# Routing by 16-bit comparisons with the row innermost, on running numbers that GpSimd writes first

## The reference

```
def _L0_ffn_ref(x, Wr, br, W1, b1, W2, b2):
    logits = jnp.einsum('bsd,de->bse', x, Wr) + br
    _, top_idx = jax.lax.top_k(logits, 2)
    mask = jnp.any(top_idx[..., None] == jnp.arange(num_experts), axis=-2)
    weights = jax.nn.softmax(jnp.where(mask, logits, NEG_INF), axis=-1)
    for e in range(num_experts):
        h = jax.nn.relu(jnp.einsum('bsd,dh->bsh', x, W1[e]) + b1[e])
        y = jnp.einsum('bsh,hd->bsd', h, W2[e]) + b2[e]
        out = out + y * (weights[:, :, e] * mask[:, :, e])[:, :, None]

def _L1_ffn_ref(x, router_W, router_b, W1, b1, W2, b2):
    probs = jax.nn.softmax(x @ router_W + router_b, axis=-1)
    gates = jax.nn.one_hot(jnp.argmax(probs, axis=-1), N_EXPERTS) * probs
    h = jax.nn.relu(jnp.einsum('bsd,edf->besf', x, W1) + b1[:, None, :])
    y = jnp.einsum('besf,efd->besd', h, W2) + b2[:, None, :]
    out = jnp.einsum('bse,besd->bsd', gates, y)
```

## Time and profile before

| | us |
|---|---|
| median of 3 runs | 1454.43 |
| lowest and highest of them | 1447.27, 1460.71 |
| the profiled execution's own time | 1442.47 |
| its span in the trace, first to last instruction | 1440.8 |
| routing of layer 0, from its first Vector step to the experts' start | 480.1 to 509.2 |
| routing of layer 1, the same | 1248.4 to 1274.0 |

### The profile page before, as it was taken

How to read it: one execution, slowest core, us unless ns; L and a number is a source line. 1 busy time by engine, 2 the same in 40 slices (tenths; PEclk the granted TensorE clock), 3 DMA queues, 4 the chain that set the end, 5 groups by cost and what they waited for, 6 DMA issues and landing times. The chain is left out here.

```text
span 1440.8 us, 34643 instructions
## 1 busy us (share of the span) xinstructions
PE 1284.9 (89%) x13600; PEld 1031.4 (72%) x13600; DVE 702.2 (49%) x1744; ACT 557.9 (39%) x1246; POOL 445.0 (31%) x654
## 2 busy tenths in 40 slices
PE   5998889999998789999994999788999998479996
PEld 2666466777776479999993777556777776379996
DVE  4785445555552612222222899655666553423222
ACT  2777145555554422222221555224544454112221
POOL 5985300100000155666552222200000000135662
PEclk9999799999998799999997999689999998589998
DMA  7000111111110369999994000011111111369993
GB/s 246 2 3 2 24 30 33 38 37 37 40 40 12 131 230 339 345 347 345 344 341 114 1 1 1 12 27 40 50 44 47 43 43 27 86 219 353 358 360 146
DMA packets 61355, 177.89 MB, mean 123 GB/s; under 512 B 20608, under 2 KB 41953, under 8 KB 46756
## 3 DMA queue, kind: packets, MB, share of 16 engines
q0 software_dynamic: 22176, 141.55, 27.6%
q1 hardware_dynamic: 39044, 34.46, 9.1%
HBM read 147.62 MB, written 12.85 MB: 111 GB/s over the span
## 5 line engine op out<-in xcount | busy, mean ns | idle before, releaser
L983 DVE TENSOR_REDUCE xa_mx<-xa_ps_s 112x2 f32<-112x750 f32 x246 | 231.6, 941 | 205.0 <-PE xa_ps_s L708 201.3
L900 ACT ACTIVATE xa_p<-xa_ps_p 125x672 f32<-125x672 f32 x256 | 187.2, 731 | 248.5 <-PE xa_ps_p L714 248.5
L714 PE MATMUL xa_ps_p<-xa_qT,xa_kT 32*125 32x112 f32 x3072 | 241.7, 289 | 40.0 <-DVE xa_mx L983 23.4
L714 PEld LDWEIGHTS xa_ps_p<-xa_qT,xa_kT 32*125 32x125 f32 x3072 | 198.1, 190 | 103.2 <-ACT xa_p L900 76.9
L708 PE MATMUL xa_ps_s<-xa_kT,xa_qT 32*112 32x375 f32 x984 | 221.7, 527 | 0.1
L1850 PEld LDWEIGHTS ex_ps_h<-ex_xT,ew_w 128*128 128x128 f32 x1792 | 212.8, 195 | 4.8 <-issue 2.0
L1850 PE MATMUL ex_ps_h<-ex_xT,ew_w 128*128 128x128 f32 x1792 | 213.3, 278 | 1.3 <-ACT ex_xT L1880 1.3
L1861 PE MATMUL ex_ps_y<-ew_w,ex_hT 128*128 128x256 f32 x896 | 202.7, 379 | 0.0
L1861 PEld LDWEIGHTS ex_ps_y<-ew_w,ex_hT 128*128 128x128 f32 x896 | 165.9, 190 | 20.2
L1884 ACT ACTIVATE ex_hT<-ex_ps_h,ew_w 128x128 f32<-128x128 f32 x224 | 70.1, 364 | 252.0 <-PE ex_ps_h L1850 246.0
L1896 DVE TENSOR_SCALAR ex_hT<-ex_ps_h,ew_w 128x128 f32<-128x128 f32 x224 | 68.2, 346 | 178.9 <-PE ex_ps_h L1850 177.7
(11 more groups left out here) (315 smaller groups left out, 2006.8 us busy)
## 6 DMA issues: line engine op xcount, KB each, us to landing
xa_kT<-xa_kU SPq DMA_DIRECT2D x76, 93.8 KB
xa_kT<-kept_k SPq DMA_DIRECT2D x52, 93.8 KB
xa_qT<-xa_qU SPq DMA_DIRECT2D x64, 56.0 KB
xn<-xa_x SPq DMA_DIRECT2D x32, 112.0 KB, 2.1
lin_yg<-ys SPq DMA_DIRECT2D x16, 224.0 KB, 5.7
cT<-in_ctxT SPq DMA_DIRECT2D x4, 750.0 KB, 8.4
xa_qT<-xa_nmT SPq DMA_DIRECT2D x128, 1.8 KB
x<-in_x SPq DMA_DIRECT2D x4, 448.0 KB, 6.0
```

Source lines behind the costliest of these rows:

```text
L714: return pe.matmul(bp[0:CT, i, c * S:(c + 1) * S], kT[r:r + 32, b % RB, n, c * CT:(c + 1) * CT], qT[r:r + 32, b % RB, n, :], start=True, s ...
L900: act.activation(p[slot % 4][:, :, :], bp[0:CT, :, 0:NC3 * S], ACT.Exp).then_inc(exped, 1)
L983: dve.tensor_reduce(mx[:, b % 2, j:j + 2, n], score_banks(b, pair)[0:S, :, 0:CL], AX, ALU.max).then_inc(maxed, 1)
```

## The change

Vector now compares 16-bit numbers (BF16) with the batch row as the innermost axis: `at_place` becomes [112, k, 128, 16], `in_tile` [112, k, tiles, 16] and `token` [112, k, 2 x tiles, 16], and `atf` and `seqk` become BF16. In place of comparing a broadcast row of numbers (`place`, `tm`) with a broadcast `atf`, Pool first writes the running number into `at_place` and `in_tile` by an iota each, behind the first tile's fetch and ahead of the wait for `second_found`, and Vector compares in place, behind a new wait for `numbered`. TensorE reads the same elements as before, now 16 elements (32 bytes) apart.

```
-    g.place = sb("place", [S, SLOTS])
...
-    atf = ph.sb("atf", [S, 2, 2, NB])
-    at_place = ph.sb("at_place", [S, top * NB, SLOTS], BF16)
-    in_tile = ph.sb("in_tile", [S, top * NB, NTILE], BF16)
-    token = ph.sb("token", [S, top * NB, 2, NTILE], BF16)
+    atf = ph.sb("atf", [S, 2, 2, NB], BF16)
+    at_place = ph.sb("at_place", [S, top, SLOTS, NB], BF16)
+    in_tile = ph.sb("in_tile", [S, top, NTILE, NB], BF16)
+    token = ph.sb("token", [S, top, 2 * NTILE, NB], BF16)
...
-    seqk = ph.sb("seqk", [S, 2, NB])
+    seqk = ph.sb("seqk", [S, 2, NB], BF16)
...
-                    last = pe.matmul(bt[:, 0:2 * NTILE], at_place[:, i, :], token[:, i, :, :].rearrange("t r m -> t (r m)"),
+                    last = pe.matmul(bt[:, 0:2 * NTILE], at_place[:, k, :, b], token[:, k, :, b],
...
             fetch(0)
+            for k in range(top):
+                pool.iota(at_place[:, k], [[1, SLOTS], [0, NB]], base=0, channel_multiplier=0,
+                          allow_small_or_imprecise_dtypes=True).then_inc(numbered, 1)
+                pool.iota(in_tile[:, k], [[1, NTILE], [0, NB]], base=0, channel_multiplier=0,
+                          allow_small_or_imprecise_dtypes=True).then_inc(numbered, 1)
             pool.wait_ge(ew.second_found, 1)
...
-                ks = slice(k * NB, (k + 1) * NB)
-                dve.tensor_tensor(at_place[:, ks, :], place[:, :].unsqueeze(1).to_broadcast([S, NB, SLOTS]),
-                                  atf[:, 1, k, :].unsqueeze(2).to_broadcast([S, NB, SLOTS]), ALU.is_equal)
-                link(dve.tensor_tensor(in_tile[:, ks, :], tm[0:S, :].unsqueeze(1).to_broadcast([S, NB, NTILE]),
-                                       atf[:, 0, k, :].unsqueeze(2).to_broadcast([S, NB, NTILE]), ALU.is_equal))
-                dve.tensor_scalar(token[:, ks, 0, :], in_tile[:, ks, :], part[0:S, 0:1], None, ALU.mult)
-                dve.tensor_tensor(token[:, ks, 1, :], in_tile[:, ks, :], seqk[:, k, :].unsqueeze(2).to_broadcast([S, NB, NTILE]),
+                dve.wait_ge(numbered, 2 * (k + 1))
+                dve.tensor_tensor(at_place[:, k], at_place[:, k], atf[:, 1, k, :].unsqueeze(1).to_broadcast([S, SLOTS, NB]),
+                                  ALU.is_equal)
+                link(dve.tensor_tensor(in_tile[:, k], in_tile[:, k], atf[:, 0, k, :].unsqueeze(1).to_broadcast([S, NTILE, NB]),
+                                       ALU.is_equal))
+                dve.tensor_scalar(token[:, k, 0:NTILE], in_tile[:, k], part[0:S, 0:1], None, ALU.mult)
+                dve.tensor_tensor(token[:, k, NTILE:2 * NTILE], in_tile[:, k], seqk[:, k, :].unsqueeze(1).to_broadcast([S, NTILE, NB]),
                                   ALU.mult).then_inc(listed, 1)
```

More of the change, by code:

```diff
@@ L1086, in _ @@
                 for out, pattern, step in ((g.thr[:, :, :], [[0, NE], [SLOTS, NT // SLOTS]], 0), (g.tm[:, :], [[1, expert_tiles(2)]], 0),
-                                           (g.part[:, :], [[0, 1]], 1), (g.place[:, :], [[1, SLOTS]], 0), (g.seq[:, :], [[1, NB]], 0)):
+                                           (g.part[:, :], [[0, 1]], 1), (g.seq[:, :], [[1, NB]], 0)):
                     pool.iota(out, pattern, base=0, channel_multiplier=step, allow_small_or_imprecise_dtypes=True)
@@ L1556, in route @@
         "chain", "chosen", "counted", "expd", "weighed", "listed", "located", "stored")
-    spare_set, rows_set = ph.sem("spare_set", "rows_set")
+    spare_set, rows_set, numbered = ph.sem("spare_set", "rows_set", "numbered")
     one_hot_sum = rowx
-    lg, em8, thr, tm, part, place, seq, before = g.lg, g.em8, g.thr, g.tm[:, 0:NTILE], g.part, g.place, g.seq, g.before
+    lg, em8, thr, tm, part, seq, before = g.lg, g.em8, g.thr, g.tm[:, 0:NTILE], g.part, g.seq, g.before
     bkeys = [ph.ps(f"k{i}", [P, 512]) for i in range(4)]
```

## The result

The changed kernel takes 1459.09 us (median of 11 runs, 1445.39 to 1471.56), the kernel before 1447.27 in the same comparison (11 runs, 1438.88 to 1463.96). The ratio is 1.007, with a 95% interval of 1.0038 to 1.0101: slower, by 5 to 15 us. In this ratio and in every other comparison of times here, runs more than 1.5% above the fastest of their kernel are left out. The profiled execution took 1455.76 us, its span is 1454.0.

A forecast was written before the change was run, and what follows sets the result against it. Layer 0's routing was taken as bound by Vector's chain with TensorE right behind: 2.2 us late, 3.3 saved, gain 1.1 with waits; layer 1 nothing. From the median 1454.43 that gave 1453.3 us, range 1442 to 1463.

The forecast's parts named there:

- The hold: Layer 0 routing: Vector's softmax step L1688 waits for Pool's first large iota to end, 2.2 us late.
- The lists: Vector's 16-bit comparisons save 1.66 us a choice: 3.3 us in layer 0, 1.3 in layer 1.
- first product: TensorE in layer 0's routing: the first list, ready at 495.65 before, would be ready at 496.2.
- The product: TensorE's 16 matmuls on a list in routing, taken to stay at 0.71 us.
- rival (c): TensorE reads elements 32 bytes apart more slowly in both products: +0.3 us at 1.4 each, +4.8 at 3.7; chance 0.2.
- Layer 1: Layer 1's routing gains nothing: Pool's first gather waits for the gate weights' DMA until 1266.12 either way.
- Rival (b): Layer 0, L1688 and L1710: Pool's iotas hold Vector longer than its lists save, up to 3.9 us slower; chance 0.15.

The follow-up runs named there:

- gaps: Changed kernel, but Pool waits for each iota's end before starting the next; ratio to the kernel before 1.0026 (0.9981 to 1.0070).
- one iota: Changed kernel, but only the first iota stands in Pool's first pause, three come behind its second fetch; ratio to before 1.0105 (1.0031 to 1.0179).
- two inputs: Changed kernel, but Vector's softmax step (ex + 1) and te128 take their constant from a tile as second input; ratio to before 1.0036 (1.0003 to 1.0069).
- fours: Changed kernel with layer 0's numbers written early and rows in groups of four (elements 8 bytes apart); ratio to before 0.9991 (0.9953 to 1.0029).
- fewer keys: The kernel with fours, but one row's keys fewer ahead of TensorE's first product and one fewer between the products; ratio to before 1.0006 (0.9970 to 1.0043).

## Why the prediction was wrong, step by step

It forecast a gain of 1.1 us in layer 0; there was a loss of 6.6. By its own steps, measured to Vector's copy of the lists, which came at 501.44 and now at 510.42 - 2.42 = 508.00:

- **The hold, mis-sized: the step that failed.** "Held until then, it is 2.2 us late", with the first large iota's end as "then". That Pool's writing would hold this step was right, and the iotas were even shorter than forecast (2.5 us, 3.0 taken). But the hold lasted through all four iotas: 5.56 - 0.17 = 5.4 us. The runs with gaps and with one iota give what the prediction assumed for a single instruction, 1.7 us, and show why it was not so here: the prediction treated the iotas as four instructions with an opening behind each, and back to back there is none. Its row pair had one memset and could not show that.
- **The lists, right.** 1.22 us was forecast at 1.35, 0.44 at 0.37. From `seqk` to the first product it is 501.47 - 498.99 = 2.48 where it was 495.65 - 491.52 = 4.13: 1.65 us saved a choice, 1.66 forecast. That the sum fits so well is luck: the two misses cancel.
- **So the first product** came 5.4 - 1.65 later, less 0.3 for a wait for TensorE's counts that the hold covers: 3.4 (501.47 - 2.42 - 495.65).
- **The product, taken at 0.71 us.** This was rival (c), between 0.71 and 3.7 with a chance of 0.2, and came out at 2.3. Both products stand on TensorE's path, so 1.6 each. By itself this was enough to turn the gain into a loss: without the hold, routing was still 1.3 us longer (two inputs).
- **A term that wasn't there: the clock.** The prediction held TensorE busy throughout. Idle for 3.58 us, it went to half clock, and first product and keys together took 508.01 - 501.47 = 6.54 us in place of 3.31, of which the product accounts for 1.6 and the keys for 1.6.
- **The sum:** 3.4 + 3.2 - 0.67 (a wait that was there before) is 5.96, the second product's delay; with its own 1.6, less the 1.0 us that the copy came behind the product's end before (501.44 - 500.34 = 1.10, now 0.11), it makes 6.56: the 508.00 measured.
- **Layer 1, right.** The gate weights' DMA covers it in both traces of the changed kernel (the first gather waits its last 1.00 and 3.07 us for it); the same stretch was 24.4 and 26.7 us in them, 25.6 before.

Rival (b), the slower one, named the place, and asked for iotas of over 3.5 us there. They took 2.5; it was their row without gaps that made the hold longer than the lists' gain. The outcome is (b)'s place and (c)'s product together, which the prediction added up only for its range. That 1459.09 us lies in that range, 1442 to 1463, is no credit to the forecast: the range's upper end is those two rivals', its lower end the spread of three runs, and the direction was wrong.

On the hold, the Trainium skill (SBUF — State Buffer, Who interferes with whom) has the ports that a Vector step in a two-port mode shares with Pool taken by whoever issues first, for the whole instruction, and spares a two-input step where Pool only writes. The trace agrees with the second (0.18 us beside an iota) and goes beyond the first: 5.56 us, four instructions. The slow product is what the Trainium skill (Advanced Engine Details and Errata, SBUF Cachelines) warns of, in direction; here 16 matmuls took 0.71 and 2.3 us with both operands' elements 2 and 32 bytes apart, and 1.24 at 8.

## What to carry to other kernels

Ahead of work moved to a neighbouring engine's pause, look at what the engine that shares its ports does in that time, and count the whole row of instructions as one hold unless there is a wait between them. A second input in place of a constant took the step out of the hold here. A layout chosen for one engine is read by another: price the reader with it. And when a chain gets shorter, look for the fixed order (here the keys) that was made for its old length: in the traces, moving the keys gave routing 2.7 us where the faster comparisons without the hold had given 0.6 (fours). Moving the keys in the kernel before was not tried.

## What the runs showed of the hardware that was not expected

- A TENSOR_SCALAR of Vector over 16 elements under four back-to-back iotas was held to the last one's end (5.56 us); with a wait between the iotas a gap of 0.07 us let it in (1.70). A RECIPROCAL (0.25 us) and a TENSOR_REDUCE (0.27) beside an iota were not held.
- The trace of the kernel before has a shorter hold already: the first `seqk` took 0.38 us in place of 0.17, to 491.90, which is where Pool's issue of a weight fetch ended (490.96 + 0.94, the line below). No run tries this by itself, and in the changed kernel a `seqk` within such an issue took 0.17.

```profile
490.96 0.94 POOL L1630 DMA_INDIRECT ew_w<-in_experts0b,ew_rows  x1 [0.30 <-issue]
```

- TensorE with weights and a moving operand of 70 BF16 elements 32 bytes apart: 2.30 us for 16 matmuls at full clock in place of 0.71, and nearly the same at half (2.37).
- Vector writing BF16 elements 32 bytes apart: 8.82 us for 2048 in place of 2.29.
- An iota of 2048 BF16 elements took 2.49 us in runs of 16 equal numbers and 4.45 in runs of 4 that an outer axis repeats four times. The tile's row in the kernel with fewer keys:

```profile
L1641 POOL IOTA num<- x1: 4452/4452/4452, 1249.8 to 1249.8; 112x2048 bf16 x1
```
